# A local-attention decoder: the window mask is added by VectorE on the way to SBUF, not by mask matmuls in PSUM

## The chip, the cores and the metric

One core of a Trainium2 chip runs the whole decoder. The time is device microseconds of one execution; the figure of a kernel is the median of its runs. The engines named here are TensorE (PE, matmuls and transposes), VectorE (DVE), ScalarE (ACT), GpSimd (POOL) and SyncE (SP, which issues the DMAs). Each runs its own list of instructions in order, and they meet by semaphores.

## The reference, cut to what matters

The input is 4 sequences of 512 tokens with 128 channels. A self-attention and a cross-attention come first; they are not touched. Then six layers of local attention and a gated FFN run, and there the change is. Per layer:

```
def attn_layer(x, Wqkv, qs, ksc, Wo):            # 16 heads of 64, window 32
    q, k, v = split(x @ Wqkv)
    q = l2norm(q) * qs;  k = l2norm(k) * ksc     # then rotary, with a scale
    out = local_attention(q, k, v)
    return out @ Wo

def local_attention(q, k, v):
    # windows of 32 queries; keys: the window before and the own one, 64
    mask = (it < jb) | (it > jb + w) | (jb == -1)
    sim = einsum('bhwie,bhwje->bhwij', bq, bk2) * QK_SCALE      # QK_SCALE = 8
    sim = where(mask, -max, sim)
    attn = softmax(sim, -1)
    return einsum('bhwij,bhwje->bhwie', attn, bv2)

x = attn_layer(shift_tokens(x), ...) + x
x = ffn_layer(shift_tokens(x), ...) + x          # layernorm, W1, gelu gate, W2
```

The mask has the same pattern for every window: of the 64 keys, query r may see keys r to r + 32. In the first window of a sequence the 32 keys of the window before don't exist and are masked as well.

## The kernel before

The layers work on tiles of 128 tokens: 4 sequences x 4 tiles x 6 layers = 96 tiles, in this order. A loop `for t in range(STEPS)` of 102 steps is written out on every engine, with tiles at different stages in one step: in step t the k and q projections and the v projection belong to tile t, turning q and k to the feature-major layout and the scores to tile t - 1, turning the probabilities and the values to tile t - 2, turning the output to tile t - 3. So the work of one step on TensorE is, in the order of its queue: `project("k", t)`, `turn_out(t - 3)`, `turn("q", t - 1)`, `turn("k", t - 1)`, `project("q", t)`, `turn_probs(t - 2)`, `scores(t - 1)`, `values(t - 2)`, `project_v(t)`.

From step 6 on each step also has one piece of a finished sequence of 512 tokens, in a period of four steps: output projection ("wo", TensorE L1382 and VectorE's addition L1701), the moments of the norm ("norm": mean and variance matmuls L1389, VectorE's centring L1691, ScalarE's Ln and Exp for rstd, L1565 and L1568, behind `exps`), the hidden layer ("hidden": VectorE L1682 and ScalarE L1552 before it, matmuls L1401, three gelus L1530 between two loads of tables, three gates L1662) and the second FFN matmul ("y": L1411 and VectorE's addition L1708).

PSUM has eight banks, used as four slots of two banks. `plan` gives each result a slot in the order of use; a slot is taken again when the reader of the result before has freed it (`take`, `emptied`). Slot 3 goes from the turned k to the scores and, in hidden steps, to a part of the hidden layer. Slot 2 goes from the turned output to q, then to wo, var, the first hidden part or y, and so to the next step's turned output.

The scores of a tile are [128 queries, 16 heads x 64 keys] in two banks. Before the change, two bf16 matmuls (L1322) per tile write the mask into them: `mask_sel` (which row of the mask goes to which query, with another choice for the first tile of a sequence) times `mask` (64 rows with 0 or -1e30). 64 small matmuls (L1327) then accumulate q k onto it. VectorE's `shift_scores` reads the sum from PSUM twice: the maximum of each head (L1634), then the difference `dif` into SBUF (L1637), which frees the slot. ScalarE's `exps` (L1504) waits for that.

VectorE's queue in one step is: `sums` (L1643, L1647), `cosine_part`, `sum_squares` and `sine_part` of k (L1602, L1593, L1614), the same of q, `shift_scores(t - 1)`, `scale_out(t - 2)` (L1654, which writes what `turn_out` turns in the next step), then the piece's own additions or gates.

ScalarE's queue is: square of k (L1471), `copy_out` (L1519), `copy_q`, `copy_k` (L1497), square of q, `copy_probs`, `inverse_norm` of k and of q (L1480, L1483), `copy_v`, `exps(t - 1)`, then Ln and Exp of the norm or the gelus.

GpSimd carries the last 32 keys of the tile before (`carry`, L1259) and then, for k and for q (`rotate`), bounds the norms (L1267), adds the sine part (L1270) and scales by the norm (L1273); both last ones read and write SBUF only. At the start of a layer it also makes the cosine table (L1250), VectorE the sine table (L1626).

## Time and profile before

| | |
|---|---|
| median of 3 runs | 2109.46 us (2109.21 to 2124.83) |
| profiled execution | 2109.2 us, its span 2107.4 us |
| TensorE busy | 1964.4 us (93%) |
| VectorE busy | 1525.9 us (72%) |
| ScalarE busy | 1311.2 us (62%) |
| GpSimd busy | 995.1 us (47%) |
| mean granted TensorE clock | 0.971 |

The span goes from the first to the last instruction. Busy time is that of instructions on the engine; waiting on semaphores is not in it. The ends of matmuls are modelled. The layers begin at about 411 us and fill the rest.

### The profile page before, as it was taken

Reading aid. Unit: us, or ns where it says so; the run is one execution under the profiler, and the core shown is the slowest. Engines: PE = TensorE matmul, PEld = TensorE weight load, DVE = VectorE, ACT = ScalarE, POOL = GpSimd, SP = SyncE. Lnnn points to the kernel's source line nnn. Section 1 sums busy time; section 2 is a strip of 40 time slices with the busy share of each in tenths; the row PEclk is TensorE's granted clock in tenths of the full one; section 3 lists DMA queues with packets and bytes.
Section 4 is the critical chain, followed back from the end, with each engine's and each line's share of the span. In section 5 each row is a group of like instructions: output and inputs, shape, how many; then the busy total and the mean of one; then the engine's idle time right before and its main releaser. Section 6 shows DMA issues by size and latency. Waiting matters only on the chain.

```text
span 2107.4 us, 46811 instructions
## 1 busy us (share of the span) xinstructions
PE 1964.4 (93%) x19020; PEld 1159.9 (55%) x19020; DVE 1525.9 (72%) x1744; ACT 1311.2 (62%) x1857; POOL 995.1 (47%) x722
## 2 busy tenths in 40 slices
PE   6499887779999999999999999999999999999996
PEld 3122133356666666666666666666666666666663
DVE  4599526477877778777877787777877787778762
ACT  3077764456666667666766676666766676667662
POOL 7000004165656555555555565555555565556540
PEclk9599998899999999999999999999999999999998
DMA  4320000044334344333443344533444333343330
GB/s 112 75 54 11 2 32 5 26 121 112 96 101 108 104 127 121 101 99 101 126 113 99 99 111 121 131 93 92 119 121 121 99 89 102 101 117 104 98 104 23
DMA packets 102453, 194.55 MB, mean 92 GB/s; under 512 B 12480, under 2 KB 32448, under 8 KB 102112
## 3 DMA queue, kind: packets, MB, share of 16 engines
q1 hardware_dynamic: 102240, 191.56, 34.6%
q8 instruction: 152, 2.49, 0.5%
q14 instruction: 61, 0.50, 0.1%
HBM read 123.77 MB, written 54.66 MB: 85 GB/s over the span
## 4 chain that ended last, share of the span: by engine, by line
PE 76%; ACT 2%; issue 1%; POOL 1%; DVE 0%; DMA 0%; SPq 0%; ACTq 0%; POOLq 0%
PE ps L1297 16%; PE ps L1372 9%; PE ps L1327 8%; PE ps L1349 8%; PE ps L1382 8%; PE ps L1306 8%; PE ps L1401 6%; PE ps L1360 4%; PE ps L1337 4%; PE ps L1411 3%; PE ps L1322 2%; ACT l_v_tok L1463 1%; PE ps L1389 1%; POOL l_rot L1270 0%; POOL l_rot L1273 0%
## 5 line engine op out<-in xcount | busy, mean ns | idle before, releaser
L1270 POOL TENSOR_TENSOR l_rot<-l_rot,l_rot_s 128x1024 f32<-128x1024 f32 x192 | 455.3, 2371 | 1.0 <-DVE l_rot_s L1614 1.0
L1259 POOL COPY l_kb<-l_kb 128x512 f32<-128x512 f32 x95 | 63.1, 664 | 683.7 <-ACT l_kb L1497 683.7
L1273 POOL TENSOR_TENSOR l_rot<-l_rot,l_norms 128x1024 f32<-128x1024 f32 x192 | 365.2, 1902 | 15.0
L1602 DVE TENSOR_TENSOR l_rot<-ps,l_tab_c 128x1024 f32<-128x1024 f32 x192 | 234.9, 1223 | 164.6 <-ACT l_sq L1471 164.6
L1471 ACT ACTIVATE l_sq<-ps 128x1024 f32<-128x1024 f32 x192 | 196.8, 1025 | 204.5 <-PE ps L1297 201.9
L1614 DVE TENSOR_TENSOR l_rot_s<-ps,l_tab_s 128x512 f32<-128x512 f32 x384 | 245.3, 680 | 0.0
L1593 DVE TENSOR_REDUCE l_norms<-l_sq 128x16 f32<-128x1024 f32 x192 | 232.0, 1208 | 0.0
L1297 PE MATMUL ps<-l_wqkv,xsT 128*128 128x512 f32 x384 | 185.2, 606 | 18.2 <-ACT l_v_tok L1463 15.7
L1497 ACT ACTIVATE l_kb<-ps 64x1024 f32<-64x1024 f32 x192 | 195.7, 1019 | 1.1
L1349 PE MATMUL ps<-l_vb,l_pT 128*32 128x128 f32 x6144 | 188.6, 274 | 2.8 <-ACT l_pT L1463 1.4
L1327 PE MATMUL ps<-l_kb,l_qT 128*32 128x128 f32 x6144 | 187.6, 274 | 0.0
L1480 ACT ACTIVATE l_norms<-l_norms 128x16 f32<-128x16 f32 x192 | 41.6, 216 | 233.9 <-POOL l_norms L1267 233.9
L1297 PE MATMUL ps<-l_wqkv_odd,xsT 128*128 128x512 f32 x384 | 181.5, 595 | 4.9 <-ACT l_v_tok L1463 4.9
L1306 PE MATMUL ps<-cst,l_rot 128*128 128x128 f32 x1536 | 183.4, 273 | 0.8 <-POOL l_rot L1273 0.8
L545 ACT ACTIVATE probs<-ps 128x512 f32<-128x512 f32 x256 | 131.7, 606 | 81.2 <-PE ps L497 81.2
L1327 PEld LDWEIGHTS ps<-l_kb,l_qT 128*32 128x32 f32 x6144 | 161.8, 110 | 21.7 <-issue 21.7
L555 DVE TENSOR_REDUCE mx<-ps 128x2 f32<-128x1024 f32 x128 | 149.3, 1218 | 33.8 <-PE ps L476 33.8
L1349 PEld LDWEIGHTS ps<-l_vb,l_pT 128*32 128x32 f32 x6144 | 171.3, 110 | 4.4 <-issue 2.7
L1306 PEld LDWEIGHTS ps<-cst,l_rot 128*128 128x128 f32 x1536 | 170.7, 141 | 2.5 <-POOL l_rot L1273 2.2
L1382 PE MATMUL ps<-l_oT,l_wo 128*128 128x512 f32 x384 | 168.8, 592 | 1.2 <-ACT l_oT L1519 1.2
L1401 PE MATMUL ps<-l_xg,l_w 128*128 128x512 f32 (+1 forms) x288 | 130.8, 604 | 3.0 <-ACT l_xg L1552 3.0
L1463 ACT ACTIVATE l_v_tok<-ps 128x1024 f32<-128x1024 f32 x96 | 98.2, 1023 | 46.8 <-PE ps L1372 44.7
(172 smaller groups left out, 3170.6 us busy)
## 6 DMA issues: line engine op xcount, KB each, us to landing
l_vb<-v_scratch SPq DMA_DIRECT2D x336, 256.0 KB, 4.5
v_scratch<-l_v_tok SPq DMA_DIRECT2D x96, 512.0 KB, 4.8
l_vb<-v_scratch SPq DMA_DIRECT2D x48, 192.0 KB, 3.1
xsT<-xT SPq DMA_DIRECT2D x48, 135.8 KB, 2.5
stack<-scratch SPq DMA_DIRECT2D x96, 64.0 KB
l_xf<-xT SPq DMA_DIRECT2D x48, 128.0 KB, 2.3
l_wqkv_odd<-wqkv SPq DMA_DIRECT2D x9, 512.0 KB, 6.5
scratch<-parts SPq DMA_DIRECT2D x4, 768.0 KB, 3.7
```

Of the source, the lines that this page charges most:

```text
L1270: nc.gpsimd.tensor_tensor(rot[:, t % 2, n], rot[:, t % 2, n], rot_s[:, n], ALU.add).then_inc(added, 1)
L1273: nc.gpsimd.tensor_tensor(rot[:, t % 2, n], rot[:, t % 2, n], norms[:, t % 2, n, :, None].broadcast_to([P, HEADS, DH]), ALU.mult).then_inc ...
L1297: m = nc.tensor.matmul(slot(name, t)[:, c, :], xsT[:, b, PAD + i * P:PAD + (i + 1) * P], wqkv_sb[t // NT % 2][:, a:a + BANK], start=True, ...
L1306: m = nc.tensor.transpose(dst[:, c // 4, (c % 4) * P:(c % 4 + 1) * P], rot[:, t % 2, "qk".index(name), 2 * c:2 * c + 2, :], ident)
L1327: m = nc.tensor.matmul(dst[a:a + WINDOW, c // 4, (c % 4) * P:(c % 4 + 1) * P], qT[:, c, a:a + WINDOW], kb[:, t % 2, c, :, a:a + 2 * WINDOW ...
L1349: m = nc.tensor.matmul(dst[a:a + WINDOW, c // 4, (c % 4) * P:(c % 4 + 1) * P], pT[:, c, a:a + WINDOW], vb[:, j, :, c * DH:(c + 1) * DH], s ...
L1382: m = nc.tensor.matmul(slot("wo", b)[:, 0, :], wo_sb[:, c, :], oT[:, c, :], start=(c == 0), stop=(c == PAIRS - 1))
L1401: m = nc.tensor.matmul(slot("h", b, c)[0:n, s, :], w, xg[:, :], start=True, stop=True)
L1471: nc.scalar.activation(sq[:, 1 - r], slot(name, t).rearrange("p n (h d) -> p (n h) d", d=DH), ACT.Square).then_inc(squared, 1)
L1593: nc.vector.tensor_reduce(half, sq[:, 1 - r], AX.X, ALU.add).then_inc(summed, 1)
L1602: nc.vector.tensor_tensor(rot[:, t % 2, 1 - r], slot(name, t).rearrange("p n (h d) -> p (n h) d", d=DH), tab_c[:, 1 - r, t % TILES, None, ...
L1614: m = nc.vector.tensor_tensor(rot_s[:, 1 - r, :, a:a + H2], raw[:, :, H2 - a:DH - a], tab_s[:, 1 - r, i, None, a:a + H2] .broadcast_to([P, ...
```

## The change

`shift_scores` makes three passes instead of two. VectorE adds the mask to the scores as it moves them from PSUM to SBUF (`dif`), and this frees the slot; it then takes the maximum from `dif` and subtracts it from `dif` in place. The mask is a constant of [128, 2, 64] (the two cases of a tile), read with the heads broadcast. TensorE's two mask matmuls and their operands are gone, and the score matmuls write instead of accumulating. `exps` waits for a semaphore of its own, `shifted`, which the subtraction raises. Two casts at the start of the layers go, and the table of constants is 640 columns narrower.

```diff
--- before.py
+++ after.py
@@ -42,7 +42,7 @@
 _at = 0
 for _name, _n in (("ident", P), ("mean", P), ("sums", P), ("cosT", SEQ), ("sinT", SEQ),
                   ("kmask", HEADS), ("vmask", GROUPS * HEADS), ("ropeC", 2 * TILES * DH),
-                  ("ropeS", 2 * TILES * DH), ("wmask", 8 * 2 * WINDOW), ("wsel", 2 * P)):
+                  ("ropeS", 2 * TILES * DH), ("wmask", 2 * 2 * WINDOW)):
     CONST[_name] = (_at, _n)
     _at += _n
 N_CONST = _at
@@ -1015,8 +1015,7 @@
         vec = sb("l_vec", [P, N_VEC])
         tab_c = sb("l_tab_c", [P, 2, TILES, DH])
         tab_s = sb("l_tab_s", [P, 2, TILES, DH])
-        mask = sb("l_mask", [P, BANK], BF16)
-        mask_sel = sb("l_mask_sel", [P, 2, P], BF16)
+        mask = const("wmask").rearrange("p (a k) -> p a k", a=2)
         sq = sb("l_sq", [P, 2, HEADS, DH])
         norms = sb("l_norms", [P, 2, 2, HEADS])
         rot = sb("l_rot", [P, 2, 2, HEADS, DH])
@@ -1058,6 +1057,7 @@
 
 
         x_summed = sem("l_x_summed")
+        shifted = sem("l_scores_shifted")
         stored = [sem(f"l_stored{b}") for b in range(BATCH)]
         STEPS = ALL + 6
         SPREAD = 16 * 4
@@ -1312,21 +1312,14 @@
                     wait_free(pe, "qT", t)
                     wait_free(pe, "kT", t)
                     wait(pe, carried, t)
-                    if t == 0:
-                        pe.wait_ge(consts_set, 3)
                     take(pe, "s", t)
                     dst = slot("s", t)
-                    opening = int(t % TILES == 0)
-                    for n in range(2):
-                        rows = slice(64 * n, 64 * n + 64)
-                        nc.tensor.matmul(dst[:, n, :], mask_sel[rows, opening, :], mask[rows, :], start=True, stop=False,
-                                         skip_group_check=True)
                     for c in range(PAIRS):
                         for j in range(WINDOWS):
                             a = j * WINDOW
                             m = nc.tensor.matmul(dst[a:a + WINDOW, c // 4, (c % 4) * P:(c % 4 + 1) * P],
                                                  qT[:, c, a:a + WINDOW], kb[:, t % 2, c, :, a:a + 2 * WINDOW],
-                                                 start=False, stop=True, skip_group_check=True)
+                                                 start=True, stop=True, skip_group_check=True)
                     m.then_inc(filled("s", t), 1)
 
                 def turn_probs(t):
@@ -1476,7 +1469,7 @@
                     part = 2 * t + r
                     wait(act, bounded, part + 1)
                     if part == 0:
-                        act.wait_ge(consts_set, 3)
+                        act.wait_ge(consts_set, 1)
                     nc.scalar.activation(norms[:, t % 2, 1 - r], norms[:, t % 2, 1 - r], ACT.Ln, scale=65536.0)\
                         .then_inc(logged, 1)
                     wait(act, logged, part + 1)
@@ -1498,7 +1491,7 @@
                     m.then_inc(emptied("kT", t), 1)
 
                 def exps(t):
-                    wait_free(act, "s", t)
+                    wait(act, shifted, t + 1)
                     wait_full(act, "pT", t - 2)
                     wait(act, sum_ready, t - 1)
                     nc.scalar.activation(prob[:, t % 2], dif[:, :, :], ACT.Exp, scale=QK_SCALE).then_inc(exped, 1)
@@ -1581,10 +1574,6 @@
             @block.vector
             def _(dve):
 
-                nc.vector.tensor_copy(mask[:, :], const("wmask")).then_inc(consts_set, 1)
-                nc.vector.tensor_copy(mask_sel[:, :, :], const("wsel").rearrange("p (a q) -> p a q", a=2))\
-                    .then_inc(consts_set, 1)
-
                 def sum_squares(t, r):
 
                     part, half = 2 * t + r, norms[:, t % 2, 1 - r]
@@ -1630,13 +1619,18 @@
 
                 def shift_scores(t):
                     s = slot("s", t).rearrange("p n (h k) -> p (n h) k", k=2 * WINDOW)
+                    opening = int(t % TILES == 0)
                     wait_full(dve, "s", t)
-                    nc.vector.tensor_reduce(mx[:, t % 2, :], s, AX.X, ALU.max).then_inc(maxed, 1)
-                    wait(dve, maxed, t + 1)
                     wait(dve, exped, t)
                     nc.vector.tensor_tensor(dif[:, :, :], s,
+                                            mask[:, opening, None, :].broadcast_to([P, HEADS, 2 * WINDOW]),
+                                            ALU.add).then_inc(emptied("s", t), 1)
+                    wait_free(dve, "s", t)
+                    nc.vector.tensor_reduce(mx[:, t % 2, :], dif[:, :, :], AX.X, ALU.max).then_inc(maxed, 1)
+                    wait(dve, maxed, t + 1)
+                    nc.vector.tensor_tensor(dif[:, :, :], dif[:, :, :],
                                             mx[:, t % 2, :, None].broadcast_to([P, HEADS, 2 * WINDOW]),
-                                            ALU.subtract).then_inc(emptied("s", t), 1)
+                                            ALU.subtract).then_inc(shifted, 1)
 
                 def sums(t):
                     wait(dve, exped, t + 1)
@@ -1754,20 +1748,14 @@
         a = np.stack([tab * sc, tab * (f(1.0) / sc)])
         put(name, a.reshape(2, TILES, P, DH).transpose(2, 0, 1, 3))
 
-    m = np.zeros((P, 8, 2 * WINDOW))
+    m = np.zeros((P, 2, 2 * WINDOW))
     key = np.arange(2 * WINDOW)
-    for r in range(WINDOW):
+    for q in range(P):
+        r = q % WINDOW
         bad = (key < r) | (key > r + WINDOW)
-        m[r] = np.where(bad, -1e30, 0.0)
-        m[WINDOW + r] = np.where(bad | (key < WINDOW), -1e30, 0.0)
-    m[2 * WINDOW:] = m[:2 * WINDOW]
+        m[q, 0] = np.where(bad, -1e30, 0.0)
+        m[q, 1] = np.where(bad | ((key < WINDOW) & (q < WINDOW)), -1e30, 0.0)
     put("wmask", m)
-    s = np.zeros((P, 2, P))
-    for q in range(P):
-        s[q % WINDOW, 0, q] = 1.0
-        s[q % WINDOW + (WINDOW if q < WINDOW else 0), 1, q] = 1.0
-    s[2 * WINDOW:] = s[:2 * WINDOW]
-    put("wsel", s)
     return c
 
 
```

## Rows read from the trace of the kernel before

**Rows 1.** Busy time by stretches, mid-layers: us, busy (instructions) per engine, clock, DMA.
```profile
753.00:1026.00 273.00, 270.73 (x2935) 175.17 (x2934) 211.52 (x238) 180.91 (x244) 153.29 (x114) 1.00 0.41 109
```

**Rows 2.** Timeline of TensorE, one round: start, us, line, operation; merged runs have xcount.
```profile
1291.32 0.39 PE L1322 MATMUL ps<-l_mask,l_mask_sel 64*128 64x512 bf16 x2
...
1291.63 1.96 PE L1327 MATMUL ps<-l_kb,l_qT 128*32 128x128 f32 x64
...
1311.46 1.93 PE L1349 MATMUL ps<-l_vb,l_pT 128*32 128x128 f32 x64
...
1319.43 1.04 PE L1360 MATMUL ps<-cst,l_o_tok 128*128 128x128 f32 x8
...
1337.38 1.88 PE L1297 MATMUL ps<-l_wqkv_odd,xsT 128*128 128x512 f32 x4
```

**Rows 3.** Timeline of ScalarE, the same round.
```profile
1283.97 1.05 ACT L1504 ACTIVATE l_prob<-l_dif 128x1024 f32<-128x1024 f32 x1
...
1286.21 1.03 ACT L1471 ACTIVATE l_sq<-ps 128x1024 f32<-128x1024 f32 x1
...
1298.27 1.05 ACT L1504 ACTIVATE l_prob<-l_dif 128x1024 f32<-128x1024 f32 x1
...
1300.63 1.26 ACT L1530 ACTIVATE l_gel<-ps,l_vec 128x512 f32<-128x512 f32 x2
...
1302.44 0.68 ACT L1530 ACTIVATE l_gel<-ps,l_vec 85x512 f32<-85x512 f32 x1 [0.55 <-PE ps L1401]
...
1304.43 1.02 ACT L1471 ACTIVATE l_sq<-ps 128x1024 f32<-128x1024 f32 x1
...
1310.16 1.02 ACT L1463 ACTIVATE l_pT<-ps 128x1024 f32<-128x1024 f32 x1
```

**Rows 4.** Timeline of VectorE, the same round.
```profile
1282.21 1.22 DVE L1637 TENSOR_TENSOR l_dif<-ps,l_mx 128x1024 f32<-128x1024 f32 x1
...
1296.77 1.22 DVE L1637 TENSOR_TENSOR l_dif<-ps,l_mx 128x1024 f32<-128x1024 f32 x1
...
1315.01 1.22 DVE L1637 TENSOR_TENSOR l_dif<-ps,l_mx 128x1024 f32<-128x1024 f32 x1
...
1317.92 0.75 DVE L1708 SCALAR_TENSOR_TENSOR xT<-ps,l_vec,xT 128x512 f32<-128x512 f32 x1 [0.55 <-PE ps L1411]
```

**Rows 5.** Groups by line, VectorE: shapes, xcount, busy us, mean ns, idle before.
```profile
L1643 DVE TENSOR_REDUCE l_total<-l_prob 128x16 f32<-128x1024 f32 x96 | 116.3, 1212 | 13.0 <-ACT l_prob L1504 13.0
```

**Rows 6.** Timelines of VectorE and GpSimd where their SBUF instructions meet.
```profile
411.55 1.53 POOL L1250 TENSOR_TENSOR l_tab_c<-cst,l_scales 128x512 f32<-128x512 f32 x1
...
411.87 1.36 DVE L1585 CAST l_mask_sel<-cst 128x256 bf16<-128x256 f32 x1
...
413.15 0.41 DVE L1626 TENSOR_TENSOR l_tab_s<-cst,l_scales 128x256 f32<-128x256 f32 x1
...
1217.24 1.29 POOL L1250 TENSOR_TENSOR l_tab_c<-cst,l_scales 128x512 f32<-128x512 f32 x1
...
1218.23 0.59 DVE L1626 TENSOR_TENSOR l_tab_s<-cst,l_scales 128x256 f32<-128x256 f32 x1
...
1290.73 0.68 DVE L1682 TENSOR_TENSOR l_xg<-l_cen,l_rstd 128x512 f32<-128x512 f32 x1
...
1291.05 0.84 POOL L1259 COPY l_kb<-l_kb 128x512 f32<-128x512 f32 x1 [5.52 <-ACT l_kb L1497]
...
1309.28 0.61 POOL L1259 COPY l_kb<-l_kb 128x512 f32<-128x512 f32 x1 [8.34 <-ACT l_kb L1497]
```

**Rows 7.** Timeline of GpSimd, the round of rows 2 to 4.
```profile
1281.20 2.35 POOL L1270 TENSOR_TENSOR l_rot<-l_rot,l_rot_s 128x1024 f32<-128x1024 f32 x1
...
1283.63 1.90 POOL L1273 TENSOR_TENSOR l_rot<-l_rot,l_norms 128x1024 f32<-128x1024 f32 x1
...
1296.60 2.36 POOL L1270 TENSOR_TENSOR l_rot<-l_rot,l_rot_s 128x1024 f32<-128x1024 f32 x1
...
1314.61 2.36 POOL L1270 TENSOR_TENSOR l_rot<-l_rot,l_rot_s 128x1024 f32<-128x1024 f32 x1
```

## The prediction

> **What bounds the kernel now.** I read the busy time by stretches first, because the edit sits in a body that runs 96 times and only that body's stretch can say what one pass of it is worth. In the middle of the layers TensorE works 270.73 of 273 us at the full clock (1.00), VectorE 211.52, ScalarE 180.91, GpSimd 153.29 [rows 1]. The reader is to see a TensorE that hardly ever stops, which by itself says: less matmul work, less time. Then I read one round of four steps in order of time, engine by engine, because four steps is the period of the FFN pieces. I call the steps by their piece: norm, hidden, y, wo. TensorE ends with the wo step's next k projection at 1337.38; within the hidden step the two mask matmuls start at 1291.32 and the scores at 1291.63 [rows 2]. Second thing to see: ScalarE runs without a gap from the end of the norm step into the hidden step, and again from the hidden step's exponentials to the y step. In the norm step exps at 1283.97 is followed by the two rstd passes and, at 1286.21, by the hidden step's square of k; in the hidden step exps at 1298.27 is followed by a table load, three gelus, a table load and, at 1304.43, the y step's square of k; and that step's copy of the turned probabilities (1310.16 to 1311.18) ends 0.28 us before values starts at 1311.46 [rows 2, 3]. So two engines are at their limit there: TensorE, and a ring of ScalarE (square, copies, square, then exps) and VectorE (cosine, sum, sine, then the shift of the scores). exps waits for the end of the shift, and everything of ScalarE is queued behind it. The end of the shift is at 1283.43 in the norm step, 0.54 before exps, and at 1297.99 in the hidden step, 0.28 before it [rows 3, 4].
>
> **The change, part by part.** *Removed: the mask matmuls.* They hold TensorE for 1291.63 - 1291.32 = 0.31 us a step [rows 2]; 96 steps make 30 us at the very most, and only where TensorE sets the pace.
>
> *Removed: two casts at the start of the layers and 320 KB of constants.* One load of constants that starts in the first microseconds gets smaller; nothing in the layers waits for it any more. I count nothing (at most 1 us gained).
>
> *Added: one VectorE pass.* Now: maximum from PSUM, subtraction from PSUM. Then: addition from PSUM (as the present subtraction, 1.22 us [rows 4]), maximum from SBUF (as the sum of the probabilities, 1212 ns [rows 5]), subtraction in SBUF. Each waits for the one before it, a gap of 0.04 us, so the last one starts and ends 1.27 us later at least, in each of 96 steps. The scores' slot is free one pass after scores instead of two, about as early as now; nobody waits for it. The h part that takes it next has it in time.
>
> *Moved: the kind of the last pass.* The subtraction now has both inputs in SBUF. The trace has three such cases beside GpSimd. A cast of only 256 elements, issued at 411.87 while GpSimd's table product ran (411.55 to 413.08), took 1.36 us, to 413.23: it stood still until GpSimd was through. A VectorE product of two SBUF tensors, issued at 1218.23, took 0.59 us against 0.41 for the same instruction at 413.15, when GpSimd was idle; the GpSimd product ahead of it ended at 1218.53 (1217.24 + 1.29): blocked 0.30 us, 0.12 of it hidden in its own start-up. And the other way, GpSimd's copy issued at 1291.05, under VectorE's product of two SBUF tensors that ends at 1291.41, took 0.84 instead of 0.61 [rows 6]. All three fit one rule: whoever comes second waits for the whole instruction of the first, less some 0.12 us. The Trainium skill says this (SBUF — State Buffer, SBUF: two separate sides): VectorE with two SBUF inputs and GpSimd reading SBUF share a port pair by an exclusive lock for the whole instruction. The trace agrees, by the 1.36 us; the sum with the rule and without it are my forecast and my first rival.
>
> So I place the subtraction beside GpSimd's queue. GpSimd adds the sine part of q from 1281.20 to 1283.55 (norm), 1296.60 to 1298.96 (hidden), 1314.61 to 1316.97 (y), then scales it [rows 7]. Today's subtraction is issued at 1282.21, 1296.77 and 1315.01 [rows 4]; the new one 1.27 us later. The addition is then still running in all three. The subtraction waits for its end, runs 1.10 us beyond it (1.22 less 0.12), and GpSimd's scaling waits for it in turn (0.9 us; turning q comes over 1.3 us after it now, so I count nothing).
>
> *The sum, in one round.* Times are today's plus a shift.
> Norm: subtraction issued at 1283.48, free at 1283.55, ends at 1284.65 to 1284.78; I take 1284.78, by the unblocked end (1284.70) and 0.08. exps 1284.81 instead of 1283.97: shift 0.84, and the square of k moves to 1287.05.
> Hidden: everything of the step hangs on that square, so the shift is 0.84. Subtraction issued 1296.77 + 0.84 + 1.27 = 1298.88; GpSimd's addition ends 1298.96 + 0.84 = 1299.80; end of the subtraction 1300.90, exps 1300.93, shift 2.66. Load and two gelus move with it to 1304.55 (1301.89 now). The third gelu now waited for TensorE until 1302.44; it can start at 1304.57: shift 2.13. Square of k in the y step: 1306.56.
> y: the copy of the turned probabilities ends 1311.18 + 2.13 = 1313.31, values starts 0.15 later (my allowance for a signal, an estimate), 1313.46 instead of 1311.46: TensorE is 2.0 behind. The mask matmuls' gains before this point are lost in it. Subtraction: issued 1318.41, free 1316.97 + 2.13 = 1319.10, ends 1320.20 instead of 1316.23. The scaled output (a pass of 1.22) and the y addition (0.75), queued behind it, end at 1321.33 and 1322.00, with the starts overlapping by some 0.08. That addition frees the slot into which the wo step turns its output: start 1322.15, where TensorE (1319.43 + 2.0) is ready at 1321.43. Another 0.7: 2.7 behind [rows 2, 4].
> wo: 7 us of projection give slack to all others, so only TensorE counts: 0.31 gained. k at 1337.38 + 2.4.
> Every round costs 2.4 us. From step 7 to step 94 there are 22 whole rounds: 52.8 us. The last batch's norm and hidden steps, without GpSimd: 0.9. The first six steps have no FFN piece; the shift ends 1.8 us later there as in y, some 1 us of it before the next output is turned is slack: 3 us for four of them, an estimate from the y step. Sum 56.7. The profiled execution took 2109.2 us (its span 2107.4 and 1.8 around it), the median is 2109.46, the same within 0.02%: 2166 us.
>
> What stays unknown is the price of the block: nothing if VectorE never waits, up to 1.9 us a step if GpSimd's next instruction gets in first. I take the 0.08, 0.80 and 0.69 worked out above, by the cast and the product, which are the nearest rows.
>
> **The rivals.** *VectorE passes, GpSimd alone pays.* For it: the product at 1290.73 is not longer than those that run alone. Against it: the 1.36 us. Then the shifts are 0.76 at the hidden step's square, 1.78 at its exps (1300.05), 1.24 at the y step's square (third gelu at 1303.69), values 1312.57, that is 1.1 late; the y addition ends 1320.54, TensorE turns at 1320.69 instead of 1320.54; less 0.31 makes 0.94 a round, 20.7 us; with 1.5 for both ends 2131 us.
>
> *Faster: TensorE still sets the pace.* Point from which it decides: the ring has over 1.3 us of hidden slack in the norm and hidden steps, because ScalarE's short gap times are modelled ends. Then 96 x 0.31 = 30 us go: 2079 us. Against it stand ScalarE's unbroken queues [rows 3]: the 0.54 and 0.28 us that I see are less than one pass.
>
> *Slower still: the port is lost twice.* In the norm step the subtraction is issued 0.07 us before GpSimd's addition ends, and the scaling starts 0.08 us behind that, at 1283.63. If the subtraction comes 0.15 later, it waits for the scaling as well: GpSimd 1285.53 [rows 7], subtraction 1286.63, 1.85 later than above, with no slack in the round to take it up: 22 x 1.85 = 41 us more, 2207 us.
>
> *It does nothing measurable*: the block and the gains balance, within 1% (21 us). It needs 0.9 us a round or less, so the first rival at its lower side, or an added pass with a third of its price hidden.
>
> **How the numbers follow.** Forecast (blocked subtraction, 2145 to 2190): 0.57. GpSimd alone pays (2120 to 2140): 0.15, half of it within 1%. Port lost twice (2190 and more): 0.12. TensorE sets the pace: 0.08. Balance: 0.08. For the range I leave out the faster case and the upper part of the port case: 2124 to 2208 us. A difference under 1% is about what I call no change here. Faster 0.08, same 0.15, slower 0.77.
>
> **What the profile after would show.** The subtraction's mean: about 1.75 us over the round, 1.3 in norm steps, 2.0 in hidden and 1.8 in y steps, if blocked; 1.22 if not. GpSimd's scaling of q near 2.8 instead of 1.90, that of k unchanged. ScalarE: exps in the hidden step 2.7 us later against the round's start, and TensorE waiting ahead of values in the y step, and ahead of turning the output in the wo step. The round longer by 2.4 us; TensorE busy some 3% less of the span. VectorE's busy share up by 117 us for the pass plus the blocked time.
> I am wrong if the round's excess is in another step than y and wo's turn, if the subtraction's duration does not depend on what GpSimd runs, or if TensorE waits nowhere.

## Result and the profile after

The changed kernel takes 2175.09 us (median of 4 runs, 2159.38 to 2178.42); the kernel before, run beside it, 2114.15 us (4 runs, 2109.21 to 2124.83). The ratio over all these runs is 1.0266, with a 95% interval of 1.0222 to 1.031 (the two medians alone give 1.0288): slower, inside the forecast range and 9 us above the forecast of 2166. The profiled execution took 2178.42 us, its span 2176.6.

One thing must be taken out before terms are compared. The two attentions ahead of the layers, which the change does not touch, take a different time from execution to execution. In the two profiled executions the granted clock of TensorE differs there. The first fence is the kernel before, the second the changed one: stretch, length, busy time (instructions) of PE, PEld, DVE, ACT and POOL, granted clock, DMA.

```profile
250.00:300.00 50.00, 43.15 (x193) 14.10 (x190) 12.27 (x18) 39.21 (x72) 0.00 (x0) 1.00 0.00 0
```

```profile
250.00:300.00 50.00, 45.21 (x167) 6.55 (x160) 3.46 (x5) 28.29 (x53) 0.00 (x0) 0.58 0.00 0
```

The layers' first k projection starts at 411.5 us before and at 427.9 after; in the thirteen traces of this case it starts between 411.2 and 432.4. The runs say that this goes with the clock: of the 17 runs of the kernel before that stand beside e5 and e6 below, the shortest (2100.18 us) has a mean granted clock of 0.977 and the longest (2130.01 us) one of 0.962. Below I compare the *layers' part*, the span from that instruction to the end: 2107.4 - 411.5 = 1695.9 us before, 2176.6 - 427.9 = 1748.7 us after. The change costs 52.8 us there. I also compare the *round*, from one first k projection after a wo step to the next, in the value that most rounds of a kernel have: 68.24 us before, 70.37 after. (In every kernel some rounds are longer than that value, in the kernel before by up to 0.9 us and the last two by 2.2, so rounds alone do not add up to the whole.)

The layers' part is not quite free of the clock either. Its 22 whole rounds run at a granted clock of 1.00 in every kernel here but e4, and they are the cleanest measure: 1507.6 us before (517.45 to 2025.05), 1554.1 after (539.27 to 2093.39), 46.5 more. At both ends the traces differ. The third step of the layers takes 14.39 us at a clock of 1.00 before and 16.06 at 0.81 after, against 15.25 at 1.00 in e3, which makes the same VectorE passes and has the mask matmuls besides. The stretch behind the last whole round is 79.8 to 85.2 us long over the thirteen traces, 79.8 and 79.9 where its first 75 us have a clock of 0.93 and 85.2 where they have 0.86. So a few us of difference between two layers' parts may not be the edit's.

The page of the changed kernel, its busy shares and the engines' shares of the chain that ended last:

```profile
PE 1983.1 (91%) x18828; PEld 1144.1 (53%) x18828; DVE 1681.7 (77%) x1838; ACT 1318.5 (61%) x1857; POOL 1079.3 (50%) x722
...
PE 28%; DVE 21%; ACT 20%; issue 11%; POOL 0%; DVEq 0%; DMA 0%; ACTq 0%; SPq 0%; POOLq 0%
```

The same chain of the kernel before, and then the middle of the layers in the changed one:

```profile
PE 76%; ACT 2%; issue 1%; POOL 1%; DVE 0%; DMA 0%; SPq 0%; ACTq 0%; POOLq 0%
```

```profile
753.00:1026.00 273.00, 262.69 (x2880) 168.51 (x2879) 231.51 (x248) 180.25 (x242) 163.65 (x112) 1.00 0.40 106
```

TensorE was busy for 270.73 of these 273 us [rows 1] and now for 262.69, at the same full clock; VectorE gained 20 us of work, GpSimd 10 us of busy time although it does nothing new. Of the chain, TensorE held 76% before; now it is shared by PE, DVE and ACT: the way to the end keeps leaving TensorE for the softmax.

Where GpSimd's time comes from stands in the groups by line (count | busy, mean ns | idle before), and in one hidden step of the round that starts at 1314.76: VectorE's three passes, then GpSimd's two on q.

```profile
L1273 POOL TENSOR_TENSOR l_rot<-l_rot,l_norms 128x1024 f32<-128x1024 f32 x192 | 448.3, 2335 | 15.0
...
L1631 DVE TENSOR_TENSOR l_dif<-l_dif,l_mx 128x1024 f32<-128x1024 f32 x96 | 163.5, 1703 | 3.3
L1629 DVE TENSOR_REDUCE l_mx<-l_dif 128x16 f32<-128x1024 f32 x96 | 117.1, 1220 | 3.3
L1625 DVE TENSOR_TENSOR l_dif<-ps,cst 128x1024 f32<-128x1024 f32 x96 | 116.4, 1213 | 7.3 <-PE ps L1320 7.3
...
L1497 ACT ACTIVATE l_prob<-l_dif 128x1024 f32<-128x1024 f32 x96 | 101.5, 1057 | 151.7 <-DVE l_dif L1631 151.7
```

```profile
1341.86 1.21 DVE L1625 TENSOR_TENSOR l_dif<-ps,cst 128x1024 f32<-128x1024 f32 x1
1343.11 1.22 DVE L1629 TENSOR_REDUCE l_mx<-l_dif 128x16 f32<-128x1024 f32 x1
1344.36 2.00 DVE L1631 TENSOR_TENSOR l_dif<-l_dif,l_mx 128x1024 f32<-128x1024 f32 x1
1346.28 1.21 DVE L1648 TENSOR_TENSOR l_o_tok<-ps,l_inv 128x1024 f32<-128x1024 f32 x1
```

```profile
1342.92 2.36 POOL L1270 TENSOR_TENSOR l_rot<-l_rot,l_rot_s 128x1024 f32<-128x1024 f32 x1
1345.36 2.76 POOL L1273 TENSOR_TENSOR l_rot<-l_rot,l_norms 128x1024 f32<-128x1024 f32 x1
```

The same pair in the norm step of that round, where the two just miss each other:

```profile
1329.10 1.23 DVE L1631 TENSOR_TENSOR l_dif<-l_dif,l_mx 128x1024 f32<-128x1024 f32 x1
```

```profile
1326.83 2.35 POOL L1270 TENSOR_TENSOR l_rot<-l_rot,l_rot_s 128x1024 f32<-128x1024 f32 x1
1329.27 2.82 POOL L1273 TENSOR_TENSOR l_rot<-l_rot,l_norms 128x1024 f32<-128x1024 f32 x1
```

In the hidden step the subtraction is issued at 1344.36 while GpSimd adds; GpSimd is through at 1345.28, the subtraction ends 1.08 later, at 1346.36. GpSimd's scaling, issued at 1345.36, takes 2.76 instead of 1.90 because now it waits. In the norm step the subtraction is issued 0.08 before GpSimd's addition ends (1329.18) and takes 1.23; GpSimd's scaling, issued at 1329.27, takes 2.82. The other two take 1.79 (y, 1363.73) and 1.78 us (wo, 1379.50). exps waits for the subtraction for 151.7 us in all, against 3.3 before.

ScalarE in the same round: exps and the hidden step's square of k, then exps and the y step's square of k:

```profile
1330.36 1.06 ACT L1497 ACTIVATE l_prob<-l_dif 128x1024 f32<-128x1024 f32 x1 [0.98 <-DVE l_dif L1631]
...
1332.56 1.01 ACT L1464 ACTIVATE l_sq<-ps 128x1024 f32<-128x1024 f32 x1
...
1346.39 1.06 ACT L1497 ACTIVATE l_prob<-l_dif 128x1024 f32<-128x1024 f32 x1 [1.88 <-DVE l_dif L1631]
...
1351.90 1.03 ACT L1464 ACTIVATE l_sq<-ps 128x1024 f32<-128x1024 f32 x1
```

TensorE in the same round, where it stops (idle before, and its releaser, in brackets):

```profile
1314.76 1.88 PE L1297 MATMUL ps<-l_wqkv_odd,xsT 128*128 128x512 f32 x4
...
1329.52 1.96 PE L1297 MATMUL ps<-l_wqkv_odd,xsT 128*128 128x512 f32 x4 [0.41 <-ACT l_v_tok L1456]
1332.13 1.06 PE L1353 MATMUL ps<-cst,l_o_tok 128*128 128x128 f32 x8 [0.66 <-ACT l_rstd L1558]
...
1347.64 1.92 PE L1394 MATMUL ps<-l_xg,l_w 128*85 128x512 f32 x4 [0.81 <-DVE l_o_tok L1648]
1349.40 1.88 PE L1297 MATMUL ps<-l_wqkv_odd,xsT 128*128 128x512 f32 x4
...
1358.80 1.96 PE L1342 MATMUL ps<-l_vb,l_pT 128*32 128x128 f32 x64
...
1365.08 1.88 PE L1297 MATMUL ps<-l_wqkv_odd,xsT 128*128 128x512 f32 x4
1367.46 1.06 PE L1353 MATMUL ps<-cst,l_o_tok 128*128 128x128 f32 x8 [0.50 <-DVE xT L1702]
...
1385.13 1.88 PE L1297 MATMUL ps<-l_wqkv_odd,xsT 128*128 128x512 f32 x4
```

The first k projections of the four steps in the kernel before, whose next round starts at 1337.38 [rows 2]:

```profile
1269.13 1.88 PE L1297 MATMUL ps<-l_wqkv_odd,xsT 128*128 128x512 f32 x4
...
1284.21 1.95 PE L1297 MATMUL ps<-l_wqkv_odd,xsT 128*128 128x512 f32 x4 [0.41 <-ACT l_v_tok L1463]
...
1302.24 1.88 PE L1297 MATMUL ps<-l_wqkv_odd,xsT 128*128 128x512 f32 x4
...
1317.72 1.88 PE L1297 MATMUL ps<-l_wqkv_odd,xsT 128*128 128x512 f32 x4
```

The wait of 0.41 stands in the kernel before too. The other three are new: in the hidden step TensorE waits for ScalarE's rstd pass before it turns the output (0.66) and for VectorE's scaled output before the third h part (0.81), in the wo step for the y addition (0.50). The gaps between k projections give the steps: norm 14.76, hidden 19.88, y 15.68, wo 20.05 us, against 15.08, 18.03, 15.48 and 19.66 before: -0.32, +1.85, +0.20 and +0.39 (rounded; the round is 2.13 longer).

### The profile page after: what moved, and what is told of

It reads as the page before. It is cut to its first block, busy times and chain, and to the rows that moved or that the text cites. A ratio compares the mean times of both kernels' runs of the same rounds, so it can differ in the third digit from the quotient of the medians.

```text
span 2176.6 us, 46520 instructions
## 1 busy us (share of the span) xinstructions
PE 1983.1 (91%) x18828; PEld 1144.1 (53%) x18828; DVE 1681.7 (77%) x1838; ACT 1318.5 (61%) x1857; POOL 1079.3 (50%) x722
## 4 chain that ended last, share of the span: by engine, by line
PE 28%; DVE 21%; ACT 20%; issue 11%; POOL 0%; DVEq 0%; DMA 0%; ACTq 0%; SPq 0%; POOLq 0%
PE ps L1375 8%; ACT l_kb L1490 6%; PE ps L1297 5%; ACT l_sq L1464 5%; DVE l_mx L1629 4%; DVE l_norms L1582 4%; DVE l_rot_s L1603 4%; DVE l_dif L1625 3%; DVE l_dif L1631 3%; PE ps L1342 3%; PE ps L1306 3%; PE ps L1320 3%; PE ps L1365 3%; ACT l_oT L1512 2%; PE ps L1353 2%
## 5 line engine op out<-in xcount | busy, mean ns | idle before, releaser
L1273 POOL TENSOR_TENSOR l_rot<-l_rot,l_norms 128x1024 f32<-128x1024 f32 x192 | 448.3, 2335 | 15.0
L1297 PE MATMUL ps<-l_wqkv,xsT 128*128 128x512 f32 x384 | 188.6, 615 | 17.1 <-ACT l_v_tok L1456 14.6
L1497 ACT ACTIVATE l_prob<-l_dif 128x1024 f32<-128x1024 f32 x96 | 101.5, 1057 | 151.7 <-DVE l_dif L1631 151.7
L1631 DVE TENSOR_TENSOR l_dif<-l_dif,l_mx 128x1024 f32<-128x1024 f32 x96 | 163.5, 1703 | 3.3
```

The source lines that it names most:

```text
L1273: nc.gpsimd.tensor_tensor(rot[:, t % 2, n], rot[:, t % 2, n], norms[:, t % 2, n, :, None].broadcast_to([P, HEADS, DH]), ALU.mult).then_inc ...
L1297: m = nc.tensor.matmul(slot(name, t)[:, c, :], xsT[:, b, PAD + i * P:PAD + (i + 1) * P], wqkv_sb[t // NT % 2][:, a:a + BANK], start=True, ...
```

## Experiments

My theory is the prediction's: a third VectorE pass on the softmax ring, made longer because the subtraction now has both inputs in SBUF and meets GpSimd. The main rivals are that the third pass alone is dear, and that TensorE's own order or the masks matter more than I allowed. In the diffs "-" is the named base kernel.

**e1: no mask at all.** Base is the kernel before, without the mask matmuls (so no mask is applied) and with all else as it was.

```diff
-                    for n in range(2):
-                        rows = slice(64 * n, 64 * n + 64)
-                        nc.tensor.matmul(dst[:, n, :], mask_sel[rows, opening, :], mask[rows, :], start=True, stop=False,
-                                         skip_group_check=True)
...
-                                                 start=False, stop=True, skip_group_check=True)
+                                                 start=True, stop=True, skip_group_check=True)
```

> The kernel before without its two mask matmuls; nothing takes their place, so the mask is missing from the result. I read the layers' part, from the first k projection to the end of the span (before 1695.9 us, after 1748.7), since the attention ahead of it varies by some 16 us. My theory, two limits side by side (TensorE, and the ring of ScalarE and VectorE): 1.1 us a round of four steps, about 25 us less, 1671. If TensorE alone set the pace: 96 x 0.31 = 30 us less, 1666. If the mask matmuls were hidden: 0 to 5 us less.

Measured: 2092.8 us (4 runs), ratio to before 0.9875 (0.9807 to 0.9944). The usual round is 67.26 us, 0.98 shorter; the 22 rounds are 18.5 shorter and the layers' part is 1676.8, 19.1 shorter. Two k projections, at 1333.60 and 1400.87, show such a round. So the matmuls are worth 0.25 us of their 0.31 each as long as TensorE is the bound. The round came as expected, the total fell 6 us short of the 25: other rounds are longer than the usual one, and the third step takes 16.01 us at a clock of 0.81 where the kernel before had 14.39 at 1.00. What makes single rounds longer stays open; their clock is 1.00 as well.

**e2: the subtraction reads PSUM.** Base is the changed kernel. The addition still writes SBUF, but the maximum and the subtraction read the unmasked scores from PSUM: three passes, the last one with one input in PSUM, and no mask in the result. The scores' slot is freed by the last pass instead of the first.

```diff
-                    nc.vector.tensor_reduce(mx[:, t % 2, :], dif[:, :, :], AX.X, ALU.max).then_inc(maxed, 1)
+                    nc.vector.tensor_reduce(mx[:, t % 2, :], s, AX.X, ALU.max).then_inc(maxed, 1)
...
-                    nc.vector.tensor_tensor(dif[:, :, :], dif[:, :, :],
+                    nc.vector.tensor_tensor(dif[:, :, :], s,
```

> The kernel after with its three VectorE passes, but the maximum and the subtraction read the scores from PSUM, so that no VectorE pass of the three has two SBUF inputs. The masked scores are written and then overwritten: the mask is missing from the result. Theory of the shared port: the subtraction takes 1.22 us in all 96 steps, GpSimd's scaling of q 1.90 again, and the layers' part is 1719 us, 23 over before instead of 53 (the third pass alone: 0.94 to 1.04 us a round). Rival, the third pass is what costs and the port only stretches a wait that is there anyway: 1745 or more.

**e7: GpSimd short on q.** Base is the changed kernel. GpSimd adds and scales only 2 of the 16 heads of q (the other 14 stay unrotated and unscaled), so that it is through before the subtraction starts (in one norm step at 1308.17, with the subtraction at 1309.27). The subtraction keeps both inputs in SBUF.

```diff
+                    hs = slice(0, 2) if r == 1 else slice(0, HEADS)
+                    nc.gpsimd.tensor_tensor(rot[:, t % 2, n, hs], rot[:, t % 2, n, hs], rot_s[:, n, hs], ALU.add)\
+                        .then_inc(added, 1)
```

> The kernel after, in which GpSimd adds the sine part of q and scales q for 2 of the 16 heads only (the rest of q stays unrotated and unscaled in the result). VectorE's three passes are unchanged, two SBUF inputs and all, but GpSimd is through before the subtraction is issued. Port theory: the subtraction takes 1.22 us everywhere and the layers' part is about 1719, as in the run with the passes from PSUM. Rival, an in-place subtraction in SBUF is slow by itself: it stays near 1.7 us and the layers' part near 1749.

The groups by line, e2 first, then e7:

```profile
L1273 POOL TENSOR_TENSOR l_rot<-l_rot,l_norms 128x1024 f32<-128x1024 f32 x192 | 365.2, 1902 | 15.0
L1631 DVE TENSOR_TENSOR l_dif<-ps,l_mx 128x1024 f32<-128x1024 f32 x96 | 117.5, 1224 | 3.3
```

```profile
L1633 DVE TENSOR_TENSOR l_dif<-l_dif,l_mx 128x1024 f32<-128x1024 f32 x96 | 117.6, 1225 | 3.3
```

Measured: e2 2144.29 us (4 runs), ratio to before 1.0125 (1.0039 to 1.0211), round 69.36, layers' part 1721.1, that is 27.6 less than the changed kernel. e7 2144.24 us (one run), round 69.04, layers' part 1718.1, 30.6 less. In both the subtraction is back at 1.22 us, in e2 by its operands, in e7 by the other engine's absence; in e2 GpSimd's scaling is back at 1902 ns as well. What follows, by the 22 rounds, where the clock is the same: the meeting at SBUF is 21.5 us (e2) or 26.8 us (e7) of the 46.5, the third pass less the masks the other 25.0 or 19.7. The layers' parts give 27.6 or 30.6 of 52.8; of e2's 27.6, 4.8 lie ahead of the rounds, where its clock was the higher one (0.96 against 0.92), and 1.3 behind them. e7 also takes away most of GpSimd's own work on q, which e2 leaves. The rival that the third pass alone is dear falls.

**e3: masks twice.** Base is the changed kernel, with the mask matmuls back in. The mask then counts twice, with the same result.

```diff
+                    for n in range(2):
+                        rows = slice(64 * n, 64 * n + 64)
+                        nc.tensor.matmul(dst[:, n, :], mask_sel[rows, opening, :], mask[rows, :], start=True, stop=False,
+                                         skip_group_check=True)
...
-                                                 start=True, stop=True, skip_group_check=True)
+                                                 start=False, stop=True, skip_group_check=True)
```

> The three VectorE passes of after with the mask matmuls of before kept as well (the mask is added twice). What does their removal still bring once VectorE makes three passes? My theory: TensorE counts only in the wo step and a little in y, 0.3 to 0.4 us a round: 7 to 9 us over after, layers' part 1757. Rival, the removal is worth the same as in the kernel before: 25 to 30 over after, 1776.

Measured: 2181.56 us (one run), round 70.68 (+0.31), layers' part 1751.9 (+3.2). The 22 rounds are 6.6 us longer, the stretch behind them 2.7 shorter at a higher clock, so the layers' part understates it. The same matmuls that are worth 18.5 us over the rounds in e1 are worth 6.6 here, just under the 7 to 9 expected: all but the wo step's is hidden in TensorE's new waits. The wait before the hidden step's turn drops, in the waits of the changed kernel and then of e3 (us in all, times, longest):

```profile
PE ps L1353 <- ACT l_rstd L1558: 17.4, 23, 3.0
```

```profile
PE ps L1362 <- ACT l_rstd L1567: 10.1, 23, 2.7
```

**e4: the subtraction later.** Base is the changed kernel. VectorE scales the output and adds before it subtracts, so the subtraction comes when GpSimd is already in its second instruction on q.

```diff
+                def subtract_max(t):
+                    wait(dve, maxed, t + 1)
+                    nc.vector.tensor_tensor(dif[:, :, :], dif[:, :, :],
...
+                    if has(t - 1):
+                        subtract_max(t - 1)
```

> The kernel after with VectorE's scaled output put between the maximum and the subtraction, so that the subtraction is issued about 1.1 us later, when GpSimd has already begun to scale q. By the port's rule (who comes second waits for the whole instruction) it now waits for that scaling: it ends 1.9 to 2.0 us later than in after in the norm and hidden steps, takes up to 2.9 us, and the round is 4 to 4.8 us longer: layers' part about 1840 to 1850. Without such a rule the order costs one pass of 1.1 us ahead of exps in each of two steps, less the stretch that is gone: 1748 plus 25 to 50.

VectorE and then GpSimd in one hidden step:

```profile
1321.77 2.74 DVE L1622 TENSOR_TENSOR l_dif<-l_dif,l_mx 128x1024 f32<-128x1024 f32 x1
```

```profile
1319.10 2.36 POOL L1270 TENSOR_TENSOR l_rot<-l_rot,l_rot_s 128x1024 f32<-128x1024 f32 x1
1321.53 1.90 POOL L1273 TENSOR_TENSOR l_rot<-l_rot,l_norms 128x1024 f32<-128x1024 f32 x1
```

GpSimd's scaling, now first, takes its 1.90 us and ends at 1323.43; the subtraction ends at 1324.51, 1.08 later. The one who comes second waits, whichever engine it is. All subtractions: mean 2421 ns, longest 2.76 us. Measured: 2281.89 us (one run), layers' part 1858.4, 109.7 more than the changed kernel, against an expected 1840 to 1850, that is 91 to 101 more.

The rounds alternate, with few exceptions, between 73.38 and 76.28, 3.0 and 5.9 over the changed kernel's; 4 to 4.8 was expected of each. The difference goes with the clock: the short rounds have a granted clock of 1.00 throughout, the long ones 0.98. Below are two hidden steps, in both of which TensorE stops for 2.6 us before it turns the output. In the first, of a long round, the clock averages 0.54 over the 3 us from 1308 on, close to the lower of its two levels (1.2 of 2.4 GHz), and the two turns take 1.76 and 2.93 us. In the second, of a short round, it is 1.00 and they take 1.07 and 1.91:

```profile
1307.15 1.76 PE L1353 MATMUL ps<-cst,l_o_tok 128*128 128x128 f32 x8 [2.58 <-ACT l_rstd L1558]
1308.70 2.93 PE L1306 MATMUL ps<-cst,l_rot 128*128 128x128 f32 x16
```

```profile
1383.80 1.07 PE L1353 MATMUL ps<-cst,l_o_tok 128*128 128x128 f32 x8 [2.59 <-ACT l_rstd L1558]
1384.70 1.91 PE L1306 MATMUL ps<-cst,l_rot 128*128 128x128 f32 x16
```

These two hidden steps take 22.41 and 20.69 us, so 1.7 of the 3.3 us between these two rounds (76.64 and 73.38) arise there; the rest comes in the steps behind. Why the clock falls in every other round only stays open. The sum over the rounds met the forecast in part because of it.

**e5: rstd ahead of exps.** Base is the changed kernel. In norm steps ScalarE makes rstd while it would wait for the subtraction, and exps after it.

```diff
-                    if has(t - 1):
+                    if has(t - 1) and b_norm is None:
...
+                        if has(t - 1):
+                            exps(t - 1)
```

> The kernel after with ScalarE's two rstd passes ahead of exps in the norm step instead of behind it, nothing else. ScalarE idles 0.98 us before exps there now. By the ring (everything of ScalarE is queued behind exps and the y step's start hangs on it) the round gets 1.0 us shorter: 22 us, layers' part 1727. If the loss were instead in TensorE's slots or in VectorE's busy time, the order on ScalarE would change nothing: within 3 us of 1748.7.

Measured: 2149.37 us (4 runs), ratio to before 1.0129 (1.0069 to 1.0189); round 69.73 (-0.64), layers' part 1731.6 (-17.1 against 22 expected; the 22 rounds give 13.4 of it, and 3.4 lie behind them, at a higher clock). The round gained 0.64, not the 1.0 expected. The wait for rstd is gone from TensorE, but the scaled output is next late there: the turn starts at 1321.11, 1.99 after the k projection, where in the kernel before it was 1.80. The edit gains a little more than the norm steps cost when changed alone (0.53 a round, e8 below). That the ring bounds what is left is my reading and is not tested.

**e6, e8, e9, e10: one kind of step each.** Base is the kernel before; from tile 5 on only the wo (e6), norm (e8), hidden (e9) or y steps (e10) get VectorE's mask and three passes, the others keep their mask matmuls. The remainder tested is 1, 2, 3 and 0.

```diff
+        def by_vector(t):
+            return t % TILES == 1 and t > TILES
...
-                    for n in range(2):
+                    for n in range(0 if by_vector(t) else 2):
```

> The kernel before with the new form of the mask in the wo steps only (23 of the 96 tiles), where seven us of output projection give VectorE and ScalarE slack; all other tiles keep the mask matmuls and two passes. Theory: TensorE saves 0.31 us in each, nothing else is late: layers' part 7 us less than before, 1689. Rival, a third pass costs wherever it stands: 0 to 30 us more than before.

> The kernel before with the new form of the mask in the norm steps only (23 tiles); the others keep mask matmuls and two passes. The subtraction comes 0.07 us ahead of the end of GpSimd's addition, so it takes 1.22 to 1.3 us. exps of the norm step 0.8 us later, the hidden step's queue by 0.7, of which its own slack takes 0.3: by the ring 0.28 us a round, about 6 us over before, layers' part 1702. Rival, the 53 us of the whole change lie evenly on the four kinds of step: 13 each.

> The same in the hidden steps only. The subtraction waits for GpSimd and takes 2.0 us, exps comes 1.8 us later, the third gelu's wait for TensorE gives 0.55 of it back, and the y step begins 1.3 us late on ScalarE: by the ring 1.1 us a round, 25 us over before, layers' part 1721. Rival: 13 us, 1709.

> The same in the y steps only. The subtraction takes 1.8 us; VectorE's y addition, queued two passes behind it, frees the slot for the wo step's turned output 0.6 us after TensorE wants it: by the slots 0.6 us a round, 13 us over before, layers' part 1709; exps of the y step, 1.8 us later, costs nothing, since the wo step has slack. The four kinds alone would then add up to 6 + 25 + 13 - 9 = 35 us, less than the 53 together, because each finds the slack unused. Rival, exps alone decides: 0 to -7 us here, since ScalarE has over two us to spare.

The groups by line of the subtraction with both inputs in SBUF, for e6 and then e8, e9 and e10:

```profile
L1652 DVE TENSOR_TENSOR l_dif<-l_dif,l_mx 128x1024 f32<-128x1024 f32 x23 | 40.8, 1775 | 0.8
```

```profile
L1652 DVE TENSOR_TENSOR l_dif<-l_dif,l_mx 128x1024 f32<-128x1024 f32 x23 | 28.2, 1225 | 0.8
```

```profile
L1652 DVE TENSOR_TENSOR l_dif<-l_dif,l_mx 128x1024 f32<-128x1024 f32 x23 | 45.7, 1986 | 0.8
```

```profile
L1652 DVE TENSOR_TENSOR l_dif<-l_dif,l_mx 128x1024 f32<-128x1024 f32 x22 | 39.1, 1779 | 0.8
```

| steps changed | round (us) | against before | 22 rounds against before | layers' part against before | time, runs |
|---|---|---|---|---|---|
| wo (e6) | 67.95 | -0.29 | -6.7 | -8.8 | 2105.82, 12 |
| norm (e8) | 68.77 | +0.53 | +11.8 | +14.8 | 2136.81, 1 |
| hidden (e9) | 69.40 | +1.16 | +25.1 | +28.0 | 2158.07, 1 |
| y (e10) | 68.83 | +0.59 | +11.8 | +10.6 | 2119.54, 1 |
| all | 70.37 | +2.13 | +46.5 | +52.8 | 2175.09, 4 |

The wo step gains 0.29 of its 0.31 although its subtraction is as long as y's: 7 us of projection stand behind it. Its ratio to before is 0.993 (0.990 to 0.996; 12 runs against 17 with a median of 2122.12). This version is faster than both kernels, by 0.7% of the one before. The two medians lie 16 us apart, the layers' parts only 8.8 and the rounds 6.7; what the rest is no trace shows. The other three add to the round what the whole change adds, 0.53 + 1.16 + 0.59 - 0.29 = 1.99 of 2.13. My expectation that they would add to far less (35 us of 53), because each alone finds unused slack, was wrong: over the 22 rounds they add to 42.0 of 46.5. The layers' parts add to 44.6, and the first six steps, which none of the four changes, take 4.1 us more in the changed kernel (90.28 against 86.16): 48.7 of 52.8. The missed one is e8, 0.53 instead of 0.28. I had followed only ScalarE's queue. TensorE stops in it as well:

```profile
1303.53 1.96 PE L1303 MATMUL ps<-l_wqkv_odd,xsT 128*128 128x512 f32 x4 [0.41 <-ACT l_v_tok L1469]
1306.14 1.06 PE L1366 MATMUL ps<-cst,l_o_tok 128*128 128x128 f32 x8 [0.66 <-ACT l_rstd L1574]
```

The turn of the output needs the slot that rstd reads, and rstd is queued behind exps.

**e11: the wo and norm steps, with rstd first.** Base is e6, with norm steps added and the order of e5.

```diff
-            return t % TILES == 1 and t > TILES
+            return t % TILES in (1, 2) and t > TILES
```

> The new form of the mask in the wo and the norm steps (46 tiles), mask matmuls and two passes elsewhere, and in the norm steps ScalarE's two rstd passes ahead of exps. In norm steps exps then ends when the rstd passes ended before, so the longer way of the scores delays nobody, and TensorE keeps the 0.3 us of each mask pair. Theory: the most frequent round is 0.6 us shorter than before's 68.24, 67.65, the layers' part about 1681 or 15 us under before. Rival, the third pass in the norm step stays on the way (0.53 us a round, as measured there alone): round 68.5.

Measured: 2114.93 us (12 runs), ratio to before 0.997 (0.9936 to 1.0004), round 67.89 (67.65 expected), layers' part 1687.9 (1681 expected). The norm step's 0.31 is mostly not had: TensorE turns the output at 1299.68, 1.99 after the k projection where other steps take 1.72, since VectorE scales the output until 1299.63, behind three passes. e11 and e6 differ by less than these runs can tell.

## Why the prediction held, point by point

Right: the direction, the mechanism of the meeting at SBUF and the range. The first rival (GpSimd alone pays) is refuted by the subtraction's length; TensorE does not set the pace; and the port is not lost twice: the norm step's subtraction was issued at 1329.10, 0.08 before GpSimd was through, and got in ahead of the scaling at 1.23 us. No subtraction of the changed kernel is longer than 2.26 us, where waiting twice would make it 3.15; in e4 it waits for the scaling, but for that alone, and takes 2.74. Term by term, as shifts against the round's start:

| term | predicted | measured |
|---|---|---|
| exps, norm | 0.84 | 0.76 |
| square of k, hidden | 0.84 | 0.72 |
| exps, hidden | 2.66 | 2.49 |
| square of k, y | 2.13 | 1.84 |
| values, y | 2.0 | 1.71 |
| wo's turn of the output, further | 0.7 | 0.50 waited |
| round | 2.4 | 2.13 |
| 22 rounds | 52.8 | 46.5 |
| first six steps | 3 | 4.1 |
| seventh step, a wo step | none | 1.3 |
| behind the last whole round | 0.9 | 0.9 |
| whole | 56.7 | 52.8 |

(That the measured whole equals the predicted 22 rounds is chance.)

The mis-sized terms are small. The norm step's block was taken as 0.08 and cost nothing measurable in the subtraction; every later row carries that and some 0.2 more. The 22 rounds came 6.3 too high and the first six steps 1.1 too low. The seventh step (21.10 against 19.77 us) stands between the first six and the 22 rounds, and the sum had no term for it: 1.3. Of the 4.1 in the first six, 1.7 are the third step, whose clock was 0.81 against 1.00; the three steps behind it, all at 1.00, take 0.7 to 0.8 more each, which is what the 3 us for four had said. That the last term fits is chance, since that stretch varies by 5 us with the clock. The layers' part lands 3.9 under the sum. The median still came out 9 us above the forecast. The kernel before itself was taken at 2109.46, and its later sets of 7, 17 and 17 runs have medians of 2121.71, 2122.12 and 2119.20; I had tied the sum to a profiled execution whose part ahead of the layers was a short one, and the 16 us by which that part differs between the two profiles are more than all errors of the terms together.

Signs. The subtraction's mean is 1703 ns (about 1750 predicted), 1.23, 2.00 and 1.79 us by step (1.3, 2.0, 1.8). GpSimd's scaling of q takes 2.8 us, that of k 1.90 to 1.91. VectorE's busy time rose by 155.8 us from 1525.9: 116.4 for the pass and 96 x (1703 - 1224) ns = 46 for the block, less 1.8 for the two casts that are gone; the other 5 us of the difference I did not trace. TensorE's share fell from 93% to 91%; in the stretch of [rows 1] it fell by 3 points.

Two readings behind the rule were weak. The cast of 1.36 us, on which the prediction leans, has one input in SBUF and not two, so it is not a case of the subtraction's kind; the product (0.59 against 0.41) and GpSimd's copy are. And the product at 1290.73, named in favour of the first rival, started ahead of GpSimd's copy, so it says nothing either way. e2, e4 and e7 stand in their place.

Wrong: the place where TensorE stops. I had it keep its pace through the hidden step and stop ahead of values in the y step, and wrote that I would be wrong if the round's excess lay elsewhere. It does: 1.85 of the 2.13 are in the hidden step. Values starts 1.71 late, but TensorE had already lost 1.53 by the y step's k projection, at two slots of PSUM that I had not followed, the one that rstd reads and the one that holds the output until VectorE has scaled it. As I read the trace, these stops cost nothing on top, since ScalarE's queue would have stopped TensorE later in any case: it is 1.84 behind at the y step's square of k, straight after its table load. That the total came out by ScalarE's queue alone in the whole change, but not in e8, fits that: where ScalarE's shift is small, TensorE's own wait for rstd decides.

The Trainium skill (SBUF — State Buffer, SBUF: two separate sides) has a VectorE instruction with two SBUF inputs and a GpSimd instruction that reads SBUF take turns whole, the first to start going first. The traces agree: 1.22 us with no meeting (e7) or with an input in PSUM (e2), 2.00 behind GpSimd's addition, 2.74 behind its scaling (e4).

## What to carry over

Before an operand is moved from PSUM to SBUF to save another engine work, look at what GpSimd runs at that moment: here the meeting cost about as much as the extra pass less the saved matmuls (21.5 to 26.8 us against 25.0 to 19.7 over the 22 rounds). Work taken from a busy engine is worth its time only in the steps where that engine is the bound; the same mask matmuls were worth 0.98 us a round in the kernel before and 0.31 beside the three passes, so an edit to a loop body should be tried by kind of step, and kept where it gains. When a queue is shifted, follow also what each delayed instruction keeps in PSUM.

## What was new about the hardware

- A blocked instruction shows no wait in the trace. It is issued and looks long, and its end comes 1.08 us after the other engine's end for a pass of 1.22 us: 1345.28 to 1346.36 in the changed kernel, 1323.43 to 1324.51 in e4.
- A VectorE instruction that waits for GpSimd goes ahead of GpSimd's next one, issued 0.08 us after the first one's end (1345.28 and 1345.36): no subtraction of the changed kernel waited for two (the longest took 2.26 us), and GpSimd's scaling of q took 2.8 us instead.
- The granted clock of TensorE ahead of the layers was 1.00 in one execution and 0.58 in another over the same 50 us, and the layers began 16 us apart. A change of 10 us in a 2100 us kernel is read from the part that was touched, and there from a stretch whose clock is the same in both traces, or from many runs.
- One kernel at two clocks: in e4 TensorE stops for 2.58 and 2.59 us at the same place in two rounds. Behind the first stop its clock averages 0.54 over 3 us, behind the second it is 1.00, and the first step is 1.7 us longer.
